# A gated cross-attention and mixture-of-experts block on one core: another order of the turns, and the last group's one-hot rows made on ScalarE

## The chip, the core and the metric

The kernel runs on one NeuronCore of a Trainium2 chip. The core has TensorE (PE in the profile), VectorE (DVE), ScalarE (ACT), GpSimd (POOL) and SyncE (SP), each with an instruction stream of its own; they meet through semaphores only. The metric is device time in microseconds (us) of one launch; lower is better.

## The reference

`x` is 4 batches of 1024 rows of 256 numbers. Two residual steps follow each other:

```
x = x + tanh(g_xattn) * cross_attention(layernorm(x), ctx)      # 77 keys per batch, W and b behind it
x = x + tanh(g_ffn)   * moe(layernorm(x))
# cross_attention: softmax(q k^T / 16), masked by position, times ctx, then @ W.T + b
# moe: logits = x @ router_w.T; the best 2 of 8 experts, weights renormalised
#      g, u = x @ w_gate[e].T, x @ w_up[e].T;  y = (silu(g) * u) @ w_down[e].T
```

The kernel computes each expert only for the rows that chose it, so it needs a list of rows per expert before the second step can begin.

## The kernel before

**Stage 1, attention and routing.** The 4096 rows are cut into 8 groups of 512 rows (4 tiles of 128), two groups to a batch. The groups go through a software pipeline written out by hand, in turns that are numbered k = 0 to 7. In turn k, DVE adds the attention result of group k to its rows (`add_rows`, L893), takes the first choices of the router (`lg`, `m8`, `mi`, `oh`), and prepares the softmax of group n = k + 2 (`maxima`, `refine`, `negated_maxima`). ACT sums squares for the two layer norms (`sum_squares`, `sum_squares2`), computes the inverse square root (`inverse_sqrt`) and the exponentials of group n (`exponentials`, L607). PE does in turn k: `attention(k+1)`, the value product of a later batch (`values`, L1154), products that nothing reads (`keep_busy`, L1096, one is a 128x512 product of ones), `transpose_exp(k+2)` (L1160), `scores(k+4)` (L1118 and L1121) and `ranks(k)` (L1177 to L1181), which counts how many earlier rows chose the same expert. In turn k, POOL adds the two choices (`picks`), which `ranks` waits for, and writes the normalised rows. SP loads `x` and `xT` of later groups, and stores rows.

**The list.** For each of 64 units (32 tiles, two choices) DVE makes a one-hot matrix of the low 7 bits of the rank, times a code of the row: `at_lows` (L842) compares, `coded` (L852) multiplies. After the last turn the expert's start is added and `at_tile` (L1008) is made, a one-hot matrix over 78 list columns. PE multiplies the two (L1227) and so adds up the list, in 64 products of 78 columns. A row of the first half has a positive code and one of the second half a negative code; DVE turns the sum into a row number (`sign`, `size`, `shift`, `idx`, L1014 to L1022). POOL then gathers rows by indirect DMA (L504).

**Stage 2, the experts.** Pairs of tiles, 34 of them in this input, go through the gate, up and down products, each split in three parts of float32 precision, and are added to the output by indirect DMA (L516). This stage isn't touched by the change.

The order is fixed by the order of the code on each engine, and each engine takes its instructions strictly in turn. A DVE instruction that needs the result of an earlier one waits for it by `after(...)`. In the order of before, the last group's tail on DVE is:

```
at_lows(last_group - 1, 0, 4); share(last_group); wait counts and ranks
nti; at_lows(6, 4, 6); nts; at_lows(6, 6, 8); ntf; cum; coded(6); start; own_ranks(7); starts; ...
at_tile x3; at_lows(7, 0, 8); coded(7); at_tile
```

Of the kernel before, what the change touches and what calls it, by code (L numbers as in the profile page):

```python
# [55 lines left out]
def moe_flamingo(nc, x, xT, ctx_rows, ctxT, lens, g_x, g_f, w_rows, wT, b_row, b_col, router, weights, out):  # L56
# [3 lines left out]
    with es:  # L60
# [51 lines left out]
        code = sb("code", [P, GROUPS, TOPK, G], F16, a)  # L112
        pad_row = sb("pad_row", [P, 1], F32, a)
# [42 lines left out]
        sign = sb("sign", [P, TILES], F32, a)  # L156
        size = sb("size", [P, TILES], F32, a)
        none = sb("none", [P, TILES], F32, a)
        shift = sb("shift", [P, TILES], F32, a)
# [87 lines left out]
        low_ready = sem("low_ready")  # L247
        counts_ready = sem("counts_ready")
# [167 lines left out]
        def _(pool):  # L416
# [25 lines left out]
            gp.iota(code[:, 0:GROUPS // 2], [[G * P, GROUPS // 2], [0, TOPK], [P, G]], base=1, channel_multiplier=1, **exact)  # L442
            gp.iota(code[:, GROUPS // 2:], [[-G * P, GROUPS // 2], [0, TOPK], [-P, G]], base=-1, channel_multiplier=-1, **exact)
            gp.iota(pad_row[:], [[1, 1]], base=N + 1, channel_multiplier=1, **exact)
# [112 lines left out]
        def _(act):  # L557
# [121 lines left out]

            nc.scalar.preload_act_table_set("silu_and_others")  # L680
# [37 lines left out]
        def _(dve):  # L718
# [167 lines left out]
            for k in range(GROUPS):  # L886
# [13 lines left out]
                summed = mark(tt(out=lg1[:], in0=lg0[:], in1=sr[:, q], op=ALU.add))  # L900
                add_rows(1).then_inc(rows_added, 1)
                after(summed)
                ts(negmean2[:, q], lg1[:, :, NE], -1.0 / D, None, ALU.mult).then_inc(negmean2_ready, 1)
# [4 lines left out]
                if k == 0:  # L908
# [11 lines left out]
                    values(1)  # L920
                    after(squared)
                else:
                    share(k - 1)
                if n + 1 < GROUPS:
                    negated_means(n + 1)
# [3 lines left out]
                if k > 0:  # L929
                    own = own_ranks(k - 1)  # L930
                    at_lows(behind, 2, 4)
                    ranked = unit_ranks(k - 1, own)
                    at_lows(behind, 4, 6)
                    masked = low_bits(k - 1, ranked)
                    at_lows(behind, 6, 8)
                    low_places(k - 1, masked)
                dve.wait_ge(ssq2_ready, k + 1)
                if more:
                    dve.wait_ge(ssq_ready, n)
# [26 lines left out]
                if k < 2:  # L966
                    values(k + 2)
# [3 lines left out]
            at_lows(last_group - 1, 0, 4)  # L971
            share(last_group)
            dve.wait_ge(counts_ready, 1)

            dve.wait_ge(ranks_ready, GROUPS)
            counted = mark(ts(nti[:], L[:, COUNTS:COUNTS + NE], float(PT - 1), None, ALU.add))
            at_lows(last_group - 1, 4, 6)
# [3 lines left out]
            at_lows(last_group - 1, 6, 8)  # L981
            after(counted)
            counted = mark(v.tensor_copy(ntf[:], nts[:]))
            after(counted)
            counted = mark(v.tensor_tensor_scan(cum[:], one8[:], ntf[:], 0.0, ALU.mult, ALU.add))
            coded(last_group - 1)
            after(counted)
            begun = mark(tt(out=start[:], in0=cum[:], in1=ntf[:], op=ALU.subtract))
            dve.wait_ge(chosen, GROUPS)
            own = own_ranks(last_group)  # L990
# [3 lines left out]
            ranked = unit_ranks(last_group, own)  # L994
            after(begun)
            begun = mark(v.tensor_reduce(first[:], starts[:], axis=AX.X, op=ALU.add))
            masked = low_bits(last_group, ranked)
            high_bits = mark(v.tensor_single_scalar(high[:], rank[:], P.bit_length() - 1, ALU.logical_shift_right))
            low_places(last_group, masked)
            after(begun)  # L1000
            after(high_bits)
            after(mark(tt(out=col[:], in0=first[:], in1=high[:], op=ALU.add)))
            side = [P, CHUNK // 2, TILES, 2]
            for c in range(UNITS // CHUNK):
                if c == UNITS // CHUNK - 1:
                    at_lows(last_group, 0, CU)
# [339 lines left out]
```

## Time and profile before

| what | value |
|---|---|
| median of 3 runs | 424.16 us (423.8 to 424.55) |
| profiled execution | 426.31 us, with a span of 424.6 us |
| mean granted TensorE clock | 0.991 |
| busy shares of the span | PE 97%, DVE 74%, ACT 66%, POOL 66% |
| stage 1, to the last store of `at_tile` | 0 to 97.4 us |
| list to the first transposed tile | 97.4 to 104 us |
| stage 2 | 104 us to the end |

PE's busy time holds 152 products that nothing reads (`W<-ones`, 36.5 us), beside those written to `ET`, so its share doesn't tell what bounds stage 1. In that stage the order of the waits does. The columns of a timeline row are: start, duration, engine, line, operation, tensors, shape, count, and in brackets how long the engine sat idle before it and who released it.

### The profile page before, as it was taken

How to read it: one execution, taken by the hardware profiler on the slowest of the kernel's cores; microseconds unless marked ns; L12 is line 12 of the kernel's file. 1: busy time of each engine (PE TensorE's matmuls, PEld its weight loads, DVE VectorE, ACT ScalarE, POOL GpSimd, SP SyncE). 2: the span in 40 equal slices, each digit the busy share in tenths (PEclk: the TensorE clock that was granted, in tenths of full speed). 3: DMA queues.
4: the chain of work that ended last, by engine and by line, in shares of the span. 5: the costliest groups of instructions: out<-in, count | busy, mean ns of one | idle time of the engine just before them, and what ended most of it. 6: DMA issues, size and time to landing. Idle time of an engine off the chain costs nothing.

```text
span 424.6 us, 9945 instructions
## 1 busy us (share of the span) xinstructions
PE 410.6 (97%) x3249; PEld 378.0 (89%) x3249; DVE 314.2 (74%) x694; ACT 281.7 (66%) x569; POOL 278.8 (66%) x269
## 2 busy tenths in 40 slices
PE   7999899998999999999999999999999999999993
PEld 2887775544999999999999999999999999999993
DVE  6557999986687777677777777777777776777772
ACT  2468877513576767777767766777767677767673
POOL 7004754754367677777777776677777777677775
PEclk9899999999999999999999999999999999999998
DMA  6846967751786777733334333434333434333433
GB/s 185 298 154 203 298 204 245 260 197 48 244 215 146 167 170 170 177 64 50 59 54 62 64 62 50 61 52 63 69 57 50 63 51 66 68 53 50 63 55 64
DMA packets 34624, 50.25 MB, mean 118 GB/s; under 512 B 3846, under 2 KB 26023, under 8 KB 34599
## 3 DMA queue, kind: packets, MB, share of 16 engines
q0 software_dynamic: 13440, 19.19, 27.1%
q1 hardware_dynamic: 19815, 29.84, 22.2%
q10 hardware_dynamic: 1344, 0.92, 0.7%
q8 instruction: 11, 0.18, 0.2%
q14 instruction: 14, 0.11, 0.1%
HBM read 32.24 MB, written 17.70 MB: 118 GB/s over the span
## 4 chain that ended last, share of the span: by engine, by line
PE 47%; POOL 23%; issue 15%; DVE 7%; ACT 3%; POOLq 2%; DMA 2%; ACTq 0%; DVEq 0%
POOL out_rows L516 15%; PE GT L1247 11%; PE UP L1247 11%; PE Y L1275 10%; POOL xt L504 7%; PE S L1121 4%; PE W L1096 3%; PE O L1170 2%; PE XT L1237 2%; ACT ex L607 2%; DMA out_rows<-y,idx 1%; PE ET L1096 1%; DVE at_low L842 1%; POOLq L533 1%; POOLq L60 1%
## 5 line engine op out<-in xcount | busy, mean ns | idle before, releaser
L516 POOL DMA_INDIRECT out_rows<-y,idx x68 | 159.6, 2347 | 65.6 <-ACT y L678 52.1
L1039 DVE TENSOR_TENSOR gu<-raw,gu 128x1024 fp32r<-128x1024 f32 x70 | 85.8, 1226 | 62.3 <-ACT gu L654 58.9
L1247 PE MATMUL GT<-xtT,gu 128*128 128x256 f32 x828 | 113.6, 286 | 0.4 <-DVE gu L1039 0.4
L1247 PE MATMUL UP<-xtT,gu 128*128 128x256 f32 x828 | 110.6, 283 | 0.0
L1247 PEld LDWEIGHTS GT<-xtT,gu 128*128 128x128 f32 x828 | 103.8, 191 | 0.8 <-DVE gu L1039 0.7
L1247 PEld LDWEIGHTS UP<-xtT,gu 128*128 128x128 f32 x828 | 104.3, 192 | 0.0
L1275 PE MATMUL Y<-dn,hT 128*128 128x256 f32 x816 | 103.6, 283 | 0.0
L1275 PEld LDWEIGHTS Y<-dn,hT 128*128 128x128 f32 x816 | 100.4, 192 | 0.1
L504 POOL DMA_INDIRECT xt<-xn_rows,idx x74 | 74.3, 1004 | 29.3 <-issue 22.2
L654 ACT CAST gu<-raw 128x1024 fp32r x68 | 70.9, 1042 | 30.7 <-PE UP L1247 28.5
L1060 DVE TENSOR_TENSOR hid<-hid,UP 128x512 f32<-128x512 f32 x68 | 46.5, 684 | 9.7 <-PE UP L1247 9.7
L667 ACT ACTIVATE hid<-GT 128x512 f32<-128x512 f32 x69 | 40.9, 593 | 11.3 <-PE GT L1247 10.0
L662 ACT CAST xtT<-XT 128x512 fp32r<-128x512 f32 x36 | 21.1, 587 | 40.4 <-issue 33.6
L1039 DVE TENSOR_TENSOR hT<-hid,hT 128x512 fp32r<-128x512 f32 x68 | 46.5, 684 | 0.2
L671 ACT CAST hT<-hid 128x512 fp32r<-128x512 f32 x68 | 42.0, 618 | 1.5 <-DVE hid L1060 1.5
L1039 DVE TENSOR_TENSOR dn<-raw,dn 128x1024 fp32r<-128x1024 f32 x35 | 42.7, 1219 | 0.0
L1096 PE MATMUL W<-ones 128*128 128x512 bf16 x152 | 36.5, 390 | 1.3 <-POOL ones L419 1.1
L678 ACT ACTIVATE y<-Y,xt 128x256 f32<-128x256 f32 x68 | 32.2, 475 | 5.9 <-PE Y L1275 5.2
L658 ACT CAST dn<-raw 128x1024 fp32r x34 | 35.6, 1048 | 0.0
L1039 DVE TENSOR_TENSOR xtT<-XT,xtT 128x512 fp32r<-128x512 f32 x36 | 24.9, 691 | 10.1 <-ACT xtT L662 7.0
L473 POOL TENSOR_TENSOR picks<-oh 128x32 bf16<-128x32 bf16 x8 | 2.1, 258 | 43.0 <-DVE oh L961 43.0
L1096 PEld LDWEIGHTS W<-ones 128*128 128x128 bf16 x152 | 14.5, 100 | 17.3 <-issue 1.9
(168 smaller groups left out, 395.7 us busy)
## 6 DMA issues: line engine op xcount, KB each, us to landing
raw<-in_weights SPq DMA_DIRECT2D x32, 384.0 KB
xn_rows<-pay SPq DMA_DIRECT2D x8, 528.0 KB, 3.3
xTg<-in_xT SPq DMA_DIRECT2D x8, 512.0 KB, 3.9
xg<-in_x SPq DMA_DIRECT2D x8, 512.0 KB, 5.9
out_rows<-xg SPq DMA_DIRECT2D x8, 512.0 KB, 4.0
xt<-xn_rows,idx POOLq DMA_INDIRECT x74
out_rows<-y,idx POOLq DMA_INDIRECT x68
kr<-in_ctx_rows SPq DMA_DIRECT2D x1, 308.0 KB
```

What stands on the lines that cost most here:

```text
L504: gp.indirect_dma_start(out=xt[:, 2 * s + t, :], out_offset=None, in_=xn_rows, in_offset=bass.IndirectOffsetOnAxis(ap=idx[:, 2 * j + t:2 * ...
L516: gp.indirect_dma_start(out=out, out_offset=bass.IndirectOffsetOnAxis(ap=idx[:, 2 * j + t:2 * j + t + 1], axis=0), in_=y[:, j % 2, t, :], ...
L654: nc.scalar.copy(gu[:, 0, q], gate_up_of(e, q)).then_inc(gu_high[q], 1)
L658: nc.scalar.copy(dn[:, 0, b], down_of(e)).then_inc(dn_high, 1)
L667: nc.scalar.activation(hid[:, q].rearrange("p h t -> p (h t)"), GT[:, q], ACT.Silu).then_inc(silu_ready, 1)
L671: nc.scalar.copy(hT[:, 0, 2 * q:2 * q + 2], hid[:, q]).then_inc(hid_high, 1)
L678: nc.scalar.mul(y[:, s % 2, t], Y[:, t, 0:D], xt[:, 2 * s + t, bass.ds(e + CW, 1)]).then_inc(y_ready, 1)
L1039: return tt(out=out, in0=whole, in1=high.bitcast(F32), op=ALU.subtract)
L1060: tt(out=wide, in0=wide, in1=UP[:, q], op=ALU.mult).then_inc(hid_ready, 1)
L1096: mm(bank[:], ones[:], ones[:].unsqueeze(1).to_broadcast([P, G, P]), start=True, stop=True)
L1247: last = mm(bank[:, h * PT:(h + 1) * PT], gu[:, pw, q, c, w, h * P:(h + 1) * P], xtT[:, b, px, c], start=(h == 0 and c == 0 and n == 0), s ...
L1275: last = mm(Y[:, t, 0:D], hT[:, px, 2 * q + c, t * P:(t + 1) * P], dn[:, pw, b, q, c * D:(c + 1) * D], start=(q == 0 and c == 0 and px == ...
```

## The change

- `values` of batches 2 and 3 goes, on PE, from behind `attention` to behind `scores`; on DVE the copy of batch k + 1 goes behind `negated_maxima` of turn k (k = 0, 1, 2).
- `ranks(k)` goes from behind `scores(k+4)` to right behind `transpose_exp(k+2)`.
- The products that nothing reads: 7 and 1 in place of 4 and 3 around the first transposes; behind `attention`, none at k = 0 and 3 at k > 0 in place of 10 and 5; at the end of a turn 2 from k = 3 on, in place of 4 from k = 2 on; 13 in place of 18 behind the last `ranks`.
- On DVE `share(k-1)` goes between `lg1` and `negmean2`, and `negmean2` ahead of `add_rows(1)`; `negated_means(n+1)` and `low_places` go behind `ve`.
- In the tail, `at_lows` and `coded` of group 6 go ahead of the wait for the counts, and the chain of group 7's ranks goes first. The one-hot rows of group 7 leave DVE: ACT makes them by 8 `Square` and 8 `Relu` instructions on 128x128 elements.
- The codes are changed so that group 7 has a positive one, and the row number takes 4 DVE instructions in place of 5. Two small `iota` instructions more on POOL.

The core of the diff:

```diff
@@ ScalarE, behind the last turn
+            act.wait_ge(places_ready, GROUPS)
+            act.wait_ge(pool_consts, 4)
+            for u in range(CU):
+                nc.scalar.activation(apart[:, u], iota_p[:, :, 0], ACT.Square, bias=low_last[:, u:u + 1], scale=-1.0
+                                     ).then_inc(apart_ready, 1)
+            for u in range(CU):
+                act.wait_ge(apart_ready, u + 1)
+                last = nc.scalar.activation(at_low[:, (UNITS - CU + u) // 2, :, u % 2], apart[:, u], ACT.Relu,
+                                            bias=code_last[:, 0, u % G:u % G + 1], scale=code_last[:, 1, u % G:u % G + 1])
+            last.then_inc(last_low_ready, 1)
             nc.scalar.preload_act_table_set("silu_and_others")
@@ VectorE, turn k
                 summed = mark(tt(out=lg1[:], in0=lg0[:], in1=sr[:, q], op=ALU.add))
+                if k > 0:
+                    share(k - 1)
+                after(summed)
+                ts(negmean2[:, q], lg1[:, :, NE], -1.0 / D, None, ALU.mult).then_inc(negmean2_ready, 1)
                 add_rows(1).then_inc(rows_added, 1)
...
+                if n + 1 < GROUPS:
+                    negated_means(n + 1)
+                if k > 0:
+                    low_places(k - 1, masked)
                 coded(behind)
                 refine(n)
                 if more:
                     after(reduced)
                     negated_maxima(n)
+                if k + 1 < BATCH:
+                    values(k + 1)
@@ TensorE
-            keep_busy(4, W)
+            keep_busy(7, W)
             transpose_keys(0, M)
-            keep_busy(3, W)
+            keep_busy(1, W)
...
                 attention(k + 1)
-                if k < 2:
-                    values(k + 2)
-                keep_busy(10 if k == 0 else 5, ET)
+                if k > 0:
+                    keep_busy(3, ET)
                 if k + 2 < GROUPS:
                     transpose_exp(k + 2)
+                ranks(k)
                 if k + 4 < GROUPS:
                     scores(k + 4)
                 else:
                     keep_busy(9, W)
-                ranks(k)
-                if k >= 2:
-                    keep_busy(4, W)
+                if k + 2 < BATCH:
+                    values(k + 2)
+                if k >= BATCH - 1:
+                    keep_busy(2, W)
...
-            keep_busy(18, W)
+            keep_busy(13, W)
...
+                    if u == UNITS - CU:
+                        pe.wait_ge(last_low_ready, 1)
+                    else:
+                        pe.wait_ge(low_ready, u // CU + 1)
```

TensorE in turn 0, from behind the value product of `attention(1)` on. Before, the value product of batch 2 and ten products that nothing reads stand ahead of the transposes of `ex` (to `ET`):

```order
L1170 MATMUL O<-vw,eT 128x256
L1154 MATMUL W<-wT_sb,ctxT_sb 77x265 x2
L1096 MATMUL ET<-ones 128x512 x10
L1160 MATMUL ET<-ident,ex 77x128 x4
L1118 MATMUL S<-krow,qrow 128x384
L1121 MATMUL S<-krT,xTg 128x96 x8
L1177 MATMUL L<-carry,ones 128x32
```

The same stretch of the changed kernel:

```order
L1188 MATMUL O<-vw,eT 128x256
L1178 MATMUL ET<-ident,ex 77x128 x4
L1195 MATMUL L<-carry,ones 128x32
L1197 MATMUL L<-picks,ones 128x24
L1197 MATMUL L<-picks,ones 128x16
L1197 MATMUL L<-picks,ones 128x8
L1199 MATMUL L<-picks,tri 128x32
L1136 MATMUL S<-krow,qrow 128x384
L1139 MATMUL S<-krT,xTg 128x96 x8
L1172 MATMUL W<-wT_sb,ctxT_sb 77x265 x2
```

The transposes now stand right behind the attention, then the ranks (to `L`), the scores (to `S`) and the value product.

VectorE in the middle of turn 3 (one at a later turn reads the same up to turn 5), before; `ve` is what ACT's inverse square root waits for:

```order
L807 RECIPROCAL rw<-ed 128x4
L775 TENSOR_SCALAR negmean<-S 128x4
L778 TENSOR_REDUCE mx<-S 128x4
L782 COPY sr<-S 128x36
L813 TENSOR_TENSOR po<-oh,L 128x64
L842 TENSOR_TENSOR at_low<-iota_p,low 128x256
L818 TENSOR_REDUCE rank<-po 128x8
L842 TENSOR_TENSOR at_low<-iota_p,low 128x256
L823 TENSOR_SCALAR low_i<-rank 128x8
L842 TENSOR_TENSOR at_low<-iota_p,low 128x256
L827 CAST low<-low_i 128x8
L940 TENSOR_SCALAR ve<-ssq 128x8
```

And in the changed kernel, from `mx` on:

```order
L796 TENSOR_REDUCE mx<-S 128x4
L800 COPY sr<-S 128x36
L831 TENSOR_TENSOR po<-oh,L 128x64
L860 TENSOR_TENSOR at_low<-iota_p,low 128x256
L836 TENSOR_REDUCE rank<-po 128x8
L860 TENSOR_TENSOR at_low<-iota_p,low 128x256
L841 TENSOR_SCALAR low_i<-rank 128x8
L860 TENSOR_TENSOR at_low<-iota_p,low 128x256
L956 TENSOR_SCALAR ve<-ssq 128x8
L793 TENSOR_SCALAR negmean<-S 128x4
L845 CAST low<-low_i 128x8
L870 TENSOR_TENSOR at_low<-at_low,code 128x1024
```

Three small instructions (`rw`, `negmean`, `low`) left the stretch ahead of `ve`; two of them now stand right behind it.

VectorE in the tail of the changed kernel, from the last turn's end to the list:

```order
L860 TENSOR_TENSOR at_low<-iota_p,low 128x512 x2
L870 TENSOR_TENSOR at_low<-at_low,code 128x1024
L825 RECIPROCAL rw<-ed 128x4
L831 TENSOR_TENSOR po<-oh,L 128x64
L1001 TENSOR_SCALAR nti<-L 128x8
L836 TENSOR_REDUCE rank<-po 128x8
L1005 TENSOR_SCALAR nts<-nti 128x8
L841 TENSOR_SCALAR low_i<-rank 128x8
L1008 CAST ntf<-nts 128x8
L1011 CAST low_last<-low_i 128x8
```

`low_last`, which ACT's 16 new instructions wait for, is the sixth small instruction behind the wait for the counts, and no one-hot work of group 6 or 7 stands between that wait and `at_tile` any more.

## Rows read from the trace of the kernel before

**Rows 1.** Timeline of PE, start to the second scores:
```profile
1.06 6.74 PE L1096 MATMUL W<-ones 128*128 128x512 bf16 x24 [1.06 <-POOL ones L419]
...
9.32 0.36 PE L1105 MATMUL M<-ident,kr 85*128 85x85 f32 x2 [1.52 <-DVE kr L752]
...
10.53 3.58 PE L1121 MATMUL S<-krT,xTg 128*128 128x96 f32 x16
...
16.53 2.02 PE L1121 MATMUL S<-krT,xTg 128*128 128x96 f32 x16
```

**Rows 2.** Windows: stretch, its length, busy by engine, PEclk, DMA share, GB/s
```profile
13.00:14.00 1.00, 1.00 (x7) 1.00 (x7) 0.73 (x6) 0.16 (x1) 0.00 (x0) 0.50 1.03 373
...
96.00:98.00 2.00, 0.72 (x20) 0.59 (x17) 1.41 (x2) 0.00 (x0) 0.00 (x0) 1.00 0.03 8
```

**Rows 3.** Timeline of PE in turn 0:
```profile
29.45 0.28 PE L1169 MATMUL M<-vw,eT 77*128 77x9 f32 x2
...
32.07 1.06 PE L1154 MATMUL W<-wT_sb,ctxT_sb 128*77 128x265 f32 x4
32.96 2.32 PE L1096 MATMUL ET<-ones 128*128 128x512 bf16 x10
35.12 0.60 PE L1160 MATMUL ET<-ident,ex 128*77 128x128 f32 x4
```

**Rows 4.** Timeline of DVE, turns 0 to 4, value copy and turn starts:
```profile
29.65 0.49 DVE L858 SCALAR_TENSOR_TENSOR vw<-W,gates,bias 77x265 f32<-77x265 f32 x1 [2.68 <-PE W L1154]
...
30.61 0.16 DVE L940 TENSOR_SCALAR ve<-ssq 128x8 f32<-128x8 f32 x1
...
34.33 0.18 DVE L896 TENSOR_TENSOR lg<-M,rg 128x36 f32<-128x36 f32 x1
...
43.06 0.18 DVE L896 TENSOR_TENSOR lg<-M,rg 128x36 f32<-128x36 f32 x1
...
58.65 0.20 DVE L896 TENSOR_TENSOR lg<-M,rg 128x36 f32<-128x36 f32 x1
```

**Rows 5.** Timeline of ACT in turn 0, end of the squares of group 2:
```profile
28.42 0.19 ACT L584 ACTIVATION_READ_ACCUMULATOR squares<-xg,negmean 128x1 f32 x1
```

**Rows 6.** SP's issue of x for group 4, and x's landing time:
```profile
29.67 0.51 SPq L323 DMA_DIRECT2D xg<-in_x  x1
```
```profile
xg<-in_x SPq DMA_DIRECT2D x8, 512.0 KB, 5.9
```

**Rows 7.** Timeline of DVE in turn 4:
```profile
63.04 0.16 DVE L940 TENSOR_SCALAR ve<-ssq 128x8 f32<-128x8 f32 x1
...
64.31 0.16 DVE L798 SCALAR_TENSOR_TENSOR nb<-mx,rt 128x4 f32<-128x4 f32 x1
...
66.27 0.18 DVE L803 RECIPROCAL rg<-rs 128x4 f32<-128x4 f32 x1 [0.28 <-ACT ex L607]
```

**Rows 8.** Timeline of ACT in turn 4:
```profile
64.56 0.40 ACT L607 ACTIVATE ex<-S,nb,rt 128x77 f32<-128x77 f32 x1
```

**Rows 9.** Timeline of DVE, the tail:
```profile
89.35 0.17 DVE L976 TENSOR_SCALAR nti<-L 128x8 int32<-128x8 f32 x1 [0.73 <-PE L L1181]
...
93.13 2.24 DVE L1008 TENSOR_TENSOR at_tile<-iota_t,col 128x1248 f16<-128x1248 f16 x3
95.29 0.69 DVE L842 TENSOR_TENSOR at_low<-iota_p,low 128x1024 f16<-128x1024 f16 x1
96.01 0.69 DVE L852 TENSOR_TENSOR at_low<-at_low,code 128x1024 f16<-128x1024 f16 x1
96.62 0.80 DVE L1008 TENSOR_TENSOR at_tile<-iota_t,col 128x1248 f16<-128x1248 f16 x1
```

**Rows 10.** Timeline of PE, the list and the first tile:
```profile
97.48 0.79 PE L1227 MATMUL L<-at_tile,at_low 128*128 128x78 f16 x16 [1.28 <-DVE at_tile L1008]
...
103.93 0.66 PE L1285 MATMUL XT<-ident,xt 128*128 128x128 f32 x4
```

**Rows 11.** Groups by line and shape, ACT:
```profile
L593 ACT ACTIVATE squares<-xg,negmean 128x256 f32<-128x256 f32 x32 | 15.9, 497 | 2.9 <-DVE negmean L903 2.8
```

More of the change, by code:

```diff
@@ L112, in moe_flamingo @@
         code = sb("code", [P, GROUPS, TOPK, G], F16, a)
+        code_last = sb("code_last", [P, 2, G], F32, a)
+        low_last = sb("low_last", [P, CU], F32, a)
+        apart = sb("apart", [P, CU, P], F32, a)
         pad_row = sb("pad_row", [P, 1], F32, a)
@@ L247, in moe_flamingo @@
         low_ready = sem("low_ready")
+        apart_ready = sem("apart_ready")
+        last_low_ready = sem("last_low_ready")
         counts_ready = sem("counts_ready")
@@ L900, in _ @@
                 summed = mark(tt(out=lg1[:], in0=lg0[:], in1=sr[:, q], op=ALU.add))
-                add_rows(1).then_inc(rows_added, 1)
+                if k > 0:
+                    share(k - 1)
                 after(summed)
                 ts(negmean2[:, q], lg1[:, :, NE], -1.0 / D, None, ALU.mult).then_inc(negmean2_ready, 1)
+                add_rows(1).then_inc(rows_added, 1)
                 add_rows(2).then_inc(rows_added, 1)
@@ L919, in _ @@
                     squared = mark(ts(ssq[:, 0, G // 2:G], xmv[:, G // 2:G, 1], float(D), None, ALU.mult))
[L920 to L925, printed above, removed]
                 if more:
@@ L975, in _ @@
             dve.wait_ge(ranks_ready, GROUPS)
+            dve.wait_ge(chosen, GROUPS)
+            own = own_ranks(last_group)
             counted = mark(ts(nti[:], L[:, COUNTS:COUNTS + NE], float(PT - 1), None, ALU.add))
-            at_lows(last_group - 1, 4, 6)
+            ranked = unit_ranks(last_group, own)
             after(counted)
             counted = mark(ts(nts[:], nti[:], PT.bit_length() - 1, 1, ALU.logical_shift_right, ALU.logical_shift_left))
-            at_lows(last_group - 1, 6, 8)
+            masked = low_bits(last_group, ranked)
             after(counted)
             counted = mark(v.tensor_copy(ntf[:], nts[:]))
+            after(masked)
+            v.tensor_copy(low_last[:], low_i[:]).then_inc(places_ready, 1)
             after(counted)
             counted = mark(v.tensor_tensor_scan(cum[:], one8[:], ntf[:], 0.0, ALU.mult, ALU.add))
-            coded(last_group - 1)
+            high_bits = mark(v.tensor_single_scalar(high[:], rank[:], P.bit_length() - 1, ALU.logical_shift_right))
             after(counted)
             begun = mark(tt(out=start[:], in0=cum[:], in1=ntf[:], op=ALU.subtract))
-            dve.wait_ge(chosen, GROUPS)
-            own = own_ranks(last_group)
             after(begun)
@@ L1013, in _ @@
             listed = L[:, LIST:LIST + TILES]
[L1014 removed]
+            lower = mark(ts(lift[:], listed, 0.0, float(N // 2 - 1), ALU.is_lt, ALU.add))
             empty = mark(ts(none[:], listed, 0.0, pad_row[:], ALU.is_equal, ALU.mult))
[L1016 to L1017 removed]
+            after(lower)
+            lifted = mark(stt(out=size[:], in0=listed, scalar=1.0, in1=lift[:], op0=ALU.mult, op1=ALU.add))
             after(empty)
[L1019 to L1022 removed]
+            after(lifted)
+            tt(out=idx[:], in0=size[:], in1=none[:], op=ALU.add).then_inc(idx_ready, 1)
             empty = mark(ts(second_empty[:], L[0:1, LIST:LIST + TILES].rearrange("p (j t) -> p j t", t=2)[:, :, 1], 0.0, 16.0,
```

35 lines of the change are left out of this document (11 added, 24 removed).

## The prediction

> **What bounds the kernel now.** I read the chain of waits first. It shows stage 2 as one unbroken chain of 34 pairs, and stage 1 as a mixture of engines, so whatever ends stage 1 earlier ends the kernel earlier, as long as nothing in stage 2 hangs on a load of stage 1. The weight loads of later experts are issued once the first tiles have landed, so they move along. I then read each engine's timeline from 0 to 112 us. Three places matter.
>
> *The start.* PE runs 24 unread products to 7.8 us, sits idle for 1.52 us until the centred keys come, and then needs 3.58 us for the first scores; the second scores, the same 16 products, take 2.02 us [rows 1]. The windows say why: the granted clock is 0.50 (1.2 GHz) there [rows 2], and it is 1.00 nearly everywhere else.
>
> *Turns 0 to 2.* PE is the late engine. In turn 0 the value product of batch 2 and ten unread products lie between the attention, which ends at 32.07, and the transposes at 35.12 [rows 3]. And DVE holds back everything behind the copy of batch 1's values, for which it waits 2.68 us; `ve` comes only at 30.61 [rows 4], while the squares that it needs end at 28.61 [rows 5].
>
> *Turns 3 on.* The ring is DVE and ACT: `lg` 58.65, `ve` 63.04, `nb` 64.31, `ex` from 64.56, `rg` 66.27, and `lg` 0.29 later: 7.91 us a turn [rows 4, 7, 8]. DVE itself idles 0.28 in it, so it can't shrink much. *The tail* is a DVE chain: `nti` 89.35, `at_tile` from 93.13, then 1.33 us of one-hot rows between the third and the fourth `at_tile`, for which PE waits 1.28 [rows 9, 10].
>
> **The change part by part.**
>
> *Start.* Seven products instead of four push the end of the unread work from 7.8 to about 8.45 and cut the idle time to about 0.9; of three products behind the transposes two go. If the clock stays at 1.00, the first scores take about 2.0 in place of 3.58: 1.56 gained. Two products fewer at 0.216 each (ten take 2.16 from 32.96 to 35.12 [rows 3]), partly replaced by the wait for ACT's copy of the keys, give another 0.3. Everything behind is PE work in one row up to the attention of group 0, so both reach turn 0: 1.9. If the clock still falls, 0.35 is left. The trace bounds it from both sides: 1.52 idle, followed by the fall; 1.28 idle ahead of the last list products with the clock at 1.00 throughout [rows 2, 10]. 0.9 is on the safe side of the second, so I take 1.9 and keep 0.35 as the low end.
>
> *Turn 0.* `ve` no longer waits for the value copy: 28.7 in place of 30.6. Then, with the gaps of [rows 7, 8], `nb` at about 30.0 and `ex` of group 2 from about 30.3 to 32.0 (1.7 for four). The attention of group 1 ends at 32.07, the transposes follow at once, not at 35.12. Turn 1 starts on DVE when `oh` is written (`nb` + 1.5, and 0.4 for the moved value copy) and the attention is done: about 32.3 for 34.33, 2.0 gained.
>
> *Turn 1.* PE does transposes (0.6), ranks (0.2), scores (2.3), value product (0.9), so that attention of group 2 starts at 36.0. ACT has the squares of turn 1 done at 35.8, hence `ve` at 35.85 (four squares and a copy of `eT` behind 33.1), `nb` 37.2, `ex` to 39.1, turn 2 at 39.4 for 43.06: 3.65. *Turn 2* carries a value copy too (0.4, of which about 0.15 shows, since DVE idles only 0.28), turn 3 starts at about 47.4, and turn 4 at 55.3 for 58.65 [rows 4]: 3.4.
>
> *Turns 3 to 7.* `rw`, `negmean` and `low` leave the stretch ahead of `ve`: 0.14 + 0.15 + 0.13, less a stall of about 0.2 where `negmean2` now has only one small instruction between it and its input. So `ve` is 0.2 earlier; but `negmean` and `low` now lie ahead of `refine`, and `nb` moves back by the same 0.2. `ex` follows `nb` by 0.04 at best, where it now follows by 0.09 [rows 7, 8]. Between 0 and 0.06 a turn: I take 0.05 for 4 turns, 0.2 in all. Below nothing: if POOL, which works beside DVE, stretches them, 0.1 a turn is lost. The unread products that go here shorten PE where it waits anyhow, for `ex` and for `rows_added`; the scores come well ahead of `negmean` now. Both ends: 3.1 to 3.8 for all the turns; I take 3.5 with the last term.
>
> *Tail.* Ahead of the counts DVE now does all of group 6's one-hot rows: 0.34 + 0.34 + 0.6 from about 87.7, so that it is ready at 89.15, about when PE's ranks arrive (89.1): the first wait is covered by work that was needed anyway. `nti` to `at_tile` was 3.78 [rows 9]; group 6's one-hot rows, 0.2 + 0.49 + 0.59 on the same timeline, leave it, and about 0.2 of waiting that they covered comes back. So `at_tile` starts about 2.75 behind `po`, at 92.0 in place of 93.13. Four of them in a row at 0.72 end at 94.95; before, 97.42 [rows 9]. That is 2.47. ACT gets `low_last` at about 90.2. A `Square` has half the columns of [rows 11] (497 ns for 256); 0.83 ns a column off gives 0.39, and less 0.09 of overlap 0.3 each. A `Relu` has two pointer operands as `ex` has, 0.40 for 77 columns [rows 8], so 0.35 to 0.39 each. 8 x 0.3 + 8 x 0.37 = 5.4, so ACT ends at 95.6. PE needs it for its last 8 products only, which would start at 95.4. It costs 0.2 (0 to 0.5), so the tail gives 2.25, between 1.9 and 2.5. Were each ACT instruction as long as the 0.497 of the wide one, ACT would end at 98.1, and the tail would give nothing; that is the far end.
>
> The Trainium skill, "ScalarE: Activation LUTs", under "What ACT_TABLE_LOAD costs", gives 280 ns + 0.833 ns a column with one pointer operand, 93 ns for another and 93 ns of overlap. The trace agrees (493 ns for 256 columns by that rule; 497 in the row). By it the 16 come to 5.45 us, the same sum. Its "Rules for kernel authors" say to use VectorE for `relu` and not ScalarE, which speaks against this edit: DVE does the same rows in 1.33 us of trace time. By that rule alone the tail would get worse; the row says that ACT stands idle there, so I follow the row.
>
> *The row number.* One dependent instruction fewer on DVE, 0.2. PE goes on at 103.93 without idle time of its own behind its unread products [rows 10], so what the gather gains is hidden: 0. The gather also waits for the last store of normalised rows, which moves by the turns' gain, not by the tail's; the DMA engines were nearly idle from 96.0 on [rows 2], so it has landed in time by about 1 us.
>
> **Sum.** 1.9 + 3.5 + 2.25 = 7.65. The profiled execution would go from 426.31 to 418.7; the median lies 2.15 under the profiled time, so 416.5; I say 416.7, since the ring is full and small stalls add.
>
> **Rivals.**
>
> *The clock still falls at the start.* For it: the seven products end 0.9 ahead of the keys, still a gap, and fewer products follow. Against it: the 1.28 gap without a fall. 6.1 gained, 418.1.
>
> *The turns give back part.* x of group 4 is issued at 29.67 and lands 5.9 later, 35.6 [rows 6]; in my schedule it is needed at 36.4, 0.8 later. Group 5's is as tight, as its issue hangs on the POOL store of group 0. If loads or DVE's full row take half of the turns' gain (1.8), and ACT's row the far part of its price (1.0), 419.4.
>
> *The clock falls in the turns.* This is the slower side. The unread products go from 9 to 5 a turn or to 3 (turns 1 and 2), and PE will sit 1.1 to 1.3 us ahead of the transposes. At 1.2 GHz PE's work of a turn, 5.9 us (transposes, ranks, scores, attention), stretches by 3.58/2.02 to 10.4 and becomes the bound: 2.5 us more a turn. It decides from three turns on; over six it is +15, less 6: 433. Against it: the 1.28 of idle time at the list went by at full clock [rows 2, 10], and what is left idle in a turn is no longer.
>
> **How the numbers follow.** The forecast (7.65, with its own range 415.6 to 417.6) has 0.52; the clock fall at the start 0.24; part given back 0.13; the clock in the turns 0.06; 0.05 is left for an unseen wait that leaves about no change. About 0.2% (0.85 us) is what a measurement of this kernel can tell from no change. The first three are all faster, so 0.91 with a part of the rest; 0.03 the same; 0.06 slower. The range 415.0 to 419.8 holds the first three cases nearly whole.
>
> **What would show it.** The first scores at about 2.0 us and PEclk 1.00 from 10 to 14; turn starts (`lg`) near 30.4, 37.5, 53.4 (my 32.3, 39.4, 55.3 less 1.9); the first `at_tile` 2.75 behind `po`, four without a gap; ACT's 16 instructions in 5.4 us with no table load among them; the last list products released by ACT, not by DVE. It is wrong if PEclk shows 0.5 between 10 and 80 us, if a turn from the third on takes over 8.0 us, or if `squares` waits for a load of x.

## Result and the profile after

| | before | changed kernel |
|---|---|---|
| median of 6 runs each | 424.26 us (423.79 to 424.55) | 422.35 us (420.82 to 423.1) |
| ratio | | 0.9948, 95% interval 0.9934 to 0.9962 |
| profiled execution, its span | 426.31, 424.6 us | 420.82, 419.1 us |
| mean granted TensorE clock | 0.991 (profiled) | 0.985 (profiled), 0.980 to 0.982 in the other five |

The change gains 1.9 us, where 7.6 were forecast; 422.35 us is above the forecast's 415.0 to 419.8. All of the granted clocks are lower than before. Single executions of the kernel before have such a clock too (3 of the 64 that ran beside the experiments, 0.981 or 0.982, at 430.8 to 431.6 us); the ratios leave out executions over 1.5% above a kernel's fastest.

Timeline of PE in the changed kernel, columns as in [rows 1]:

```profile
10.70 2.03 PE L1139 MATMUL S<-krT,xTg 128*128 128x96 f32 x16
...
52.73 0.66 PE L1178 MATMUL ET<-ident,ex 128*77 128x128 f32 x4 [1.22 <-ACT ex L614]
...
53.71 2.98 PE L1139 MATMUL S<-krT,xTg 128*128 128x96 f32 x16
...
57.62 1.20 PE L1188 MATMUL O<-vw,eT 77*128 77x256 f32 x2
...
63.74 1.06 PE L1178 MATMUL ET<-ident,ex 128*77 128x128 f32 x4
...
89.88 3.08 PE L1249 MATMUL L<-at_tile,at_low 128*128 128x78 f16 x64 [1.48 <-DVE at_tile L1027]
...
98.93 0.33 PE L1307 MATMUL XT<-ident,xt 128*128 128x128 f32 x1 [0.36 <-DMA xt<-xn_rows,idx]
```

The first scores take 2.03 us, as forecast for them (3.58 in [rows 1]). But from the scores of turn 3 to the transposes of turn 4 everything on PE is long: the scores 2.98, the pair of products to `O` 1.20 where the pair before it has 0.68, the transposes 1.06 for 0.66. Ahead of that PE sat idle for 1.22 us, waiting for `ex`. The windows of the same kernel (columns as in [rows 2]) say what it is:

```profile
13.00:14.00 1.00, 1.00 (x12) 0.95 (x11) 0.93 (x8) 0.28 (x2) 0.00 (x0) 1.00 1.06 386
52.00:54.00 2.00, 1.26 (x12) 1.05 (x13) 1.62 (x11) 2.00 (x10) 1.22 (x6) 1.00 0.93 267
54.00:55.00 1.00, 1.00 (x10) 1.00 (x9) 1.00 (x4) 1.00 (x4) 1.00 (x3) 0.78 0.77 272
55.00:64.00 9.00, 9.00 (x31) 7.00 (x31) 6.33 (x42) 5.37 (x25) 6.08 (x16) 0.50 0.64 208
64.00:65.00 1.00, 1.00 (x11) 0.82 (x10) 1.00 (x4) 0.17 (x1) 0.76 (x4) 0.60 0.00 0
```

The granted clock is 0.50 (1.2 GHz) from some 54.5 to 64.8 us, and 1.00 around it. PE is busy for the whole of it, while DVE falls to 6.33 of 9 us. It begins some 1.8 us after the idle 1.22 has ended (at 52.73).

DVE in the changed kernel, turn starts (against [rows 4]) and the tail (against [rows 9]):

```profile
27.10 0.17 DVE L956 TENSOR_SCALAR ve<-ssq 128x8 f32<-128x8 f32 x1 [0.97 <-ACT squares L591]
...
30.83 0.20 DVE L914 TENSOR_TENSOR lg<-M,rg 128x36 f32<-128x36 f32 x1 [0.26 <-PE O L1188]
...
37.50 0.20 DVE L914 TENSOR_TENSOR lg<-M,rg 128x36 f32<-128x36 f32 x1
...
53.00 0.20 DVE L914 TENSOR_TENSOR lg<-M,rg 128x36 f32<-128x36 f32 x1
...
62.70 0.20 DVE L914 TENSOR_TENSOR lg<-M,rg 128x36 f32<-128x36 f32 x1 [2.29 <-PE O L1188]
...
70.98 0.20 DVE L914 TENSOR_TENSOR lg<-M,rg 128x36 f32<-128x36 f32 x1
...
85.72 0.22 DVE L831 TENSOR_TENSOR po<-oh,L 128x64 f32<-128x64 bf16 x1
...
89.01 2.96 DVE L1027 TENSOR_TENSOR at_tile<-iota_t,col 128x1248 f16<-128x1248 f16 x4
92.99 0.24 DVE L1034 TENSOR_SCALAR lift<-L 128x78 f32<-128x78 f32 x1 [1.01 <-PE L L1249]
```

The turns start at 30.83, 37.50 and 53.00, where 30.4, 37.5 and 53.4 were forecast. Then turn 4 takes 9.70 us, with DVE waiting 2.29 for PE, and turn 5 takes 8.28. `ve` of turn 0 (27.10) no longer waits for a value copy, only for the squares. In the tail the four `at_tile` stand in a row, but the first comes 3.29 behind `po`, not 2.75.

ACT in the tail of the changed kernel:

```profile
86.84 2.44 ACT L691 ACTIVATE apart<-iota_p,low_last 128x128 f32<-128x128 f16 x8 [3.27 <-DVE low_last L1011]
89.19 3.23 ACT L695 ACTIVATE at_low<-apart,code_last 128x128 f16<-128x128 f32 x8
92.43 1.28 ACT L698 ACT_TABLE_LOAD   x1
```

The 16 instructions take 5.58 us, and the table load follows them.

### The profile page after: what moved, and what is told of

Its sections match the earlier page's. It is cut to its first block, busy times and chain, and to the rows that moved or that the text cites. A ratio compares the mean times of both kernels' runs of the same rounds, so it can differ in the third digit from the quotient of the medians.

```text
span 419.1 us, 9883 instructions
## 1 busy us (share of the span) xinstructions
PE 406.4 (97%) x3211; PEld 377.1 (90%) x3211; DVE 311.4 (74%) x690; ACT 287.4 (69%) x585; POOL 280.6 (67%) x271
## 4 chain that ended last, share of the span: by engine, by line
PE 45%; POOL 24%; issue 16%; DVE 6%; DMA 3%; ACT 2%; POOLq 2%; SPq 0%; ACTq 0%; DVEq 0%
POOL out_rows L523 15%; PE GT L1269 11%; PE UP L1269 11%; PE Y L1297 10%; POOL xt L511 8%; PE W L1114 3%; PE S L1139 3%; PE O L1188 2%; PE XT L1259 2%; DMA xg<-in_x 2%; DVE xg L911 1%; DMA out_rows<-y,idx 1%; POOLq L60 1%; POOLq L540 1%; ACT ex L614 1%
## 5 line engine op out<-in xcount | busy, mean ns | idle before, releaser
L511 POOL DMA_INDIRECT xt<-xn_rows,idx x74 | 75.2, 1017 | 27.4 <-issue 22.2
L1114 PE MATMUL W<-ones 128*128 128x512 bf16 x136 | 34.4, 407 | 1.3 <-POOL ones L424 1.1
L1114 PEld LDWEIGHTS W<-ones 128*128 128x128 bf16 x136 | 13.6, 104 | 17.3 <-issue 3.7
```

Of the source, the lines that this page charges most:

```text
L511: gp.indirect_dma_start(out=xt[:, 2 * s + t, :], out_offset=None, in_=xn_rows, in_offset=bass.IndirectOffsetOnAxis(ap=idx[:, 2 * j + t:2 * ...
L1114: mm(bank[:], ones[:], ones[:].unsqueeze(1).to_broadcast([P, G, P]), start=True, stop=True)
```

## The experiments

Ratios are to the kernel before, run beside each experiment on the same chip. Undisturbed means a mean granted clock of 0.994 or more over the whole execution. The first four ran together, the next four on another chip, then two and then one on a third; across these groups the ratios are to be compared, not the times.

**The kernel before, unchanged.**

> The kernel of before, word for word, for the granted clock and the span of each run. Theory A (the profiled execution of before, 426.31, was one with the clock fall at the start, and most executions don't have it): the six runs spread by about 2 us in two groups, those at 424 with a higher mean clock than the profiled one's 0.991, and a profile of a run at 424 shows the first scores at about 2.0 us. Rival B (the start is the same each time and the profiler or the chip adds 2): every run's clock is 0.991 and the first scores take 3.6 us at 424 too.

424.88 us (424.56 to 426.3, 11 runs), ratio 0.9997 (0.9985 to 1.0009), clocks 0.996 to 0.999. The fall at the start that [rows 1, 2] show isn't there. But neither theory is right as it was put: the longer executions, 425.8 and 426.3, have a clock of 0.998 too, so something other than this fall lengthens them. PE in the profiled execution, which is the one at 426.3 (span 424.6):

```profile
4.45 4.61 PE L1096 MATMUL W<-ones 128*128 128x512 bf16 x16
9.37 0.37 PE L1105 MATMUL M<-ident,kr 85*128 85x85 f32 x2 [0.31 <-DVE kr L752]
...
10.58 2.02 PE L1121 MATMUL S<-krT,xTg 128*128 128x96 f32 x16
...
102.34 0.66 PE L1285 MATMUL XT<-ident,xt 128*128 128x128 f32 x4
```

The 24 unread products last until 9.06, not 7.80, so the gap ahead of the keys is 0.31 and not 1.52. The other four profiled executions with the old start (in four of the kernels below) have gaps from none to 1.14 there, and all have first scores of 2.02. All of stage 1 is 1.6 us earlier than in [rows 4, 10] (first transposed tile 102.34 for 103.93). Yet the span is the same 424.6. From the first down product (`Y`) to the end of the span every profiled execution of this study takes 310.0 to 310.7 us, so the 1.6 us went between the two, in what I call the opening of stage 2: first transposed tile to first `Y`. It is 10.3 us in the profiled execution of before and 12.0 here.

**Only the start's products.**

```diff
-            keep_busy(4, W)
+            keep_busy(7, W)
             transpose_keys(0, M)
-            keep_busy(3, W)
+            keep_busy(1, W)
```

> Before, with 7 and 1 unread products around the first transposes in place of 4 and 3, nothing else. If the start's term was right as a mean: 1.5 to 1.9 faster, 422.4. Theory A: only executions that would have fallen gain, so 0.2 to 0.8 faster on the median, about 423.7, with the first scores at 2.0 us and clock 0.995.

425.49 us (423.73 to 427.32, 11 runs), ratio 1.0015 (0.9998 to 1.0032). Both sizes expected, 1.5 to 1.9 and 0.2 to 0.8 us faster, are missed, and the start's term is nothing: the turns begin 0.07 to 0.14 us earlier than in the unchanged kernel's trace (turn 0 at 22.22 for 22.29, turn 4 at 56.97 for 57.08), and the time doesn't follow.

**The change with the old number of unread products in the turns and behind the last ranks.**

```diff
@@ against the changed kernel
-                    keep_busy(3, ET)
+                    keep_busy(5, ET)
...
-                    keep_busy(2, W)
+                    keep_busy(4, W)
...
-            keep_busy(13, W)
+            keep_busy(18, W)
```

> The changed kernel with the unread products of the turns as before: 5 behind attention in place of 3 (k > 0), 4 at a turn's end from k = 3 on in place of 2, 18 in place of 13 behind the last ranks. Theory A (the turns' gain is eaten by a clock fall in the turns that the thinner PE row lets in): clock 1.00 in all turns, mean clock of 0.99 or more, no turn over 8.0 us, and 418 to 419.5. Rival (the fall doesn't hang on the unread products but on the order, which bunches PE's work): the clock falls as before this edit, 421.5 to 423.

419.32 us (418.65 to 420.08, 4 runs), ratio 0.9869 (0.9855 to 0.9884), clocks 0.995 to 0.997. With this row nothing falls, and the change gains 5.5 us.

**The kernel before with fewer unread products in the turns, nothing else.**

```diff
@@ against the kernel before
-                keep_busy(10 if k == 0 else 5, ET)
+                keep_busy(10 if k == 0 else 3, ET)
...
-                if k >= 2:
-                    keep_busy(4, W)
+                if k >= 3:
+                    keep_busy(2, W)
```

> Before, with fewer unread products in the turns (3 in place of 5 from k = 1 on; none at the end of turn 2 and 2 from turn 3 on in place of 4), the order as it was. Theory A (fewer products alone let the clock fall): a stretch at 0.50 in the turns, mean clock about 0.98, 425 to 428. Rival (it takes the new order too): clock as before and 424.2 within 0.5.

429.24 us as the median of 11 runs, but from 424.13 to 436.9, with clocks from 0.999 down to 0.960; ratio 1.0063 (1.0032 to 1.0095) with the five longest left out. Nine of the eleven have a clock of 0.983 or less, at 428.8 us and above; the other two are at 424.13 and 425.17. The last wait ahead of the fall in its profiled execution (433.55 us), and the windows:

```profile
49.18 0.66 PE L1160 MATMUL ET<-ident,ex 128*77 128x128 f32 x4 [1.50 <-ACT ex L607]
```

```profile
50.00:60.00 10.00, 10.00 (x41) 8.50 (x41) 7.09 (x46) 6.77 (x30) 4.78 (x16) 0.51 0.69 222
60.00:70.00 10.00, 10.00 (x43) 8.28 (x41) 5.96 (x39) 5.34 (x22) 2.92 (x8) 0.50 0.56 186
70.00:80.00 10.00, 9.66 (x47) 6.18 (x45) 7.01 (x42) 5.78 (x26) 4.25 (x13) 0.80 0.51 164
```

No step of the change is in it but the thin row of unread products. In the old order that alone costs 4 us in four of its executions and 7 to 12 in five. The wait for `ex` is 1.50 us, where the unchanged kernel has 1.09 at this place and stays at full clock. So the thin row is enough for a fall; the next four runs were for the sizes.

**The changed kernel, unchanged.**

> The changed kernel word for word, beside the run with the old unread products (419.3) and on the same chip as this call's others. Theory A (all of what is missing is the clock in the turns): every run has a mean clock of 0.980 to 0.985, the median is 421.5 to 423, and the profile shows 8 to 14 us at 0.50 between 45 and 75 us. Rival (the first six runs were odd): clock 0.995 and 419.5.

421.72 us (8 runs), ratio 0.9923 (0.9888 to 0.9959). The runs are of two kinds: 417.85, 418.1 and 418.81 at clocks of 0.994 to 0.998, and five from 421.43 to 422.86 at 0.980 or 0.981. With the six runs of the result, 11 of 14 executions fall, by their mean clocks; that every one would, as expected, isn't so. The profiled one is undisturbed (span 417.1). PE and the windows in it:

```profile
53.03 0.66 PE L1178 MATMUL ET<-ident,ex 128*77 128x128 f32 x4 [1.21 <-ACT ex L614]
```

```profile
54.00:64.00 10.00, 9.18 (x62) 6.87 (x61) 9.52 (x53) 9.09 (x38) 7.30 (x19) 1.00 0.71 234
```

The same place, the same idle time of 1.21 us, and the clock stays at 1.00. So the gap of this length doesn't decide the fall by itself.

**Only the new order of the turns**, on PE and DVE, with the old 5 and 4 unread products, the old start and the old tail.

```diff
@@ against the kernel before, TensorE (VectorE as in the change)
-                if k < 2:
-                    values(k + 2)
-                keep_busy(10 if k == 0 else 5, ET)
+                if k > 0:
+                    keep_busy(5, ET)
...
+                ranks(k)
...
-                ranks(k)
-                if k >= 2:
+                if k + 2 < BATCH:
+                    values(k + 2)
+                if k >= BATCH - 1:
                     keep_busy(4, W)
```

> Before, with the new order of the turns on PE and DVE, the unread products of the turns at the old numbers (5, 9, 4; none in turn 0), the old start and the old tail. The forecast's term: 3.5 faster, 421.2 where before is 424.7. If stage 2's opening (gathers and weight loads side by side) takes part of what comes earlier, 2.5 or less.

419.27 us (419.02 to 419.66, 5 runs), ratio 0.9881 (0.9867 to 0.9895): 5.0 us. DVE in turn 4 of this kernel:

```profile
52.93 0.20 DVE L896 TENSOR_TENSOR lg<-M,rg 128x36 f32<-128x36 f32 x1
...
53.66 0.17 DVE L905 TENSOR_SCALAR negmean<-lg 128x4 f32<-128x4 f32 x1
...
56.75 0.16 DVE L938 TENSOR_SCALAR ve<-ssq 128x8 f32<-128x8 f32 x1
...
58.25 0.16 DVE L798 SCALAR_TENSOR_TENSOR nb<-mx,rt 128x4 f32<-128x4 f32 x1
...
60.18 0.18 DVE L803 RECIPROCAL rg<-rs 128x4 f32<-128x4 f32 x1 [0.24 <-ACT ex L607]
60.46 0.20 DVE L896 TENSOR_TENSOR lg<-M,rg 128x36 f32<-128x36 f32 x1
```

And three lines of the unchanged kernel: the same instruction in turns 3 and 4, and the wait for the scores in turn 3.

```profile
50.17 0.16 DVE L903 TENSOR_SCALAR negmean<-lg 128x4 f32<-128x4 f32 x1
...
51.82 0.16 DVE L775 TENSOR_SCALAR negmean<-S 128x4 f32<-128x4 f32 x1 [0.37 <-PE S L1121]
...
58.08 0.41 DVE L903 TENSOR_SCALAR negmean<-lg 128x4 f32<-128x4 f32 x1
```

A turn is 7.53 us, not 7.91. From `lg` to `ve` it is 3.82 for 4.39 [rows 4, 7], from `ve` to `nb` 1.50 for 1.27, and the rest is as it was. I had forecast 0.2 less and 0.2 more for the first two. I had charged a stall of 0.2 for `negmean2` with only one small instruction ahead of it; the trace has no such stall, and the instruction itself takes 0.17 where it took 0.41. It isn't the place alone that made it long: in the old order it takes 0.35 to 0.42 in five turns and 0.16 in three, in the new one 0.15 to 0.17 in all eight. In turn 3, where the old order has 0.16, DVE waits 0.37 for the scores instead, and that wait is gone too.

**Only the new tail**, with 18 unread products behind the last ranks (the edit is the tail's part of the change: VectorE, ScalarE, the codes and the wait of the last eight list products).

```diff
@@ against the kernel before
+            for u in range(CU):
+                nc.scalar.activation(apart[:, u], iota_p[:, :, 0], ACT.Square, bias=low_last[:, u:u + 1], scale=-1.0
...
+            for u in range(CU):
+                act.wait_ge(apart_ready, u + 1)
```

> Before, with the new codes and the new tail (one-hot rows of group 7 on ACT, group 6's ahead of the counts, four instructions to the row number), 18 unread products behind the last ranks, the old turns and the old start. The forecast's term: 2.25 faster, 422.5. Rival of the forecast (ACT is the late engine of the tail): 1.0 faster. If the list's last products are released by DVE at four at_tile of 0.74, ACT costs nothing.

422.25 us (421.97 to 422.96, 6 runs), ratio 0.9954 (0.9941 to 0.9967): 2.0 us. DVE and PE there:

```profile
87.89 0.22 DVE L831 TENSOR_TENSOR po<-oh,L 128x64 f32<-128x64 bf16 x1
...
91.15 2.97 DVE L1025 TENSOR_TENSOR at_tile<-iota_t,col 128x1248 f16<-128x1248 f16 x4
```

```profile
92.02 2.63 PE L1246 MATMUL L<-at_tile,at_low 128*128 128x78 f16 x56 [0.36 <-DVE at_tile L1025]
94.91 0.49 PE L1246 MATMUL L<-at_tile,at_low 128*128 128x78 f16 x8 [0.26 <-ACT at_low L695]
```

The last eight products are released by ACT and wait 0.26 for it, near the 0.2 of the forecast. This run moves the one-hot rows and reorders DVE's tail at once; no run separates the two. The first `at_tile` comes 3.26 behind `po`, and 0.42 us earlier than in the unchanged kernel (91.57). The list ends at 95.40 for 96.71, with the turns 0.06 later: 1.4 in the profiled executions, 2.0 in the medians. Where the other 0.6 lies wasn't traced.

**The change with PE's gaps filled.**

```diff
@@ against the changed kernel
-                    keep_busy(3, ET)
+                    keep_busy(3 if k == 1 else 6 if k == 2 else 8, ET)
...
-            keep_busy(13, W)
+            keep_busy(18, W)
```

> The changed kernel with 3, 6 and from turn 3 on 8 unread products behind attention, which the waits for ex (0.5 to 2.0 us) have room for, 2 at a turn's end as it is, and 18 behind the last ranks. Theory A: clock at 1.00 as with the old numbers, and 419.3 or 0.2 to 0.5 less, since PE's attention starts up to 0.4 earlier. Rival (the two at the turn's end matter, not those behind attention): the clock falls, 421 to 423.

418.79 us (417.28 to 420.61, 6 runs), ratio 0.9875 (0.9851 to 0.9898), clocks 0.995 to 0.998. PE has no idle time left over 0.2 us from 35 to 70. The turns are shorter than anywhere (last `lg` 73.74, for 74.82 in the undisturbed changed kernel), and the first transposed tile comes at 95.64. But the kernel isn't faster than that one's 417.85 to 418.81: the opening of stage 2 takes 10.8 us here and 10.2 there. The first tile is 0.64 earlier than there, but the third tile's transposes start at 104.54 in both, as its gather is waited for:

```profile
95.64 0.66 PE L1307 MATMUL XT<-ident,xt 128*128 128x128 f32 x4 [0.39 <-DMA xt<-xn_rows,idx]
...
104.54 0.65 PE L1259 MATMUL XT<-ident,xt 128*128 128x128 f32 x4 [0.99 <-DMA xt<-xn_rows,idx]
```

**The same, with the weight loads of experts 2 and 3 behind the third tile.**

```diff
@@ SyncE, against the filled kernel
-            load_weights(2, range(PARTS))
-            load_weights(3, range(PARTS))
             for s in range(2, AHEAD):
                 sp.wait_ge(tile_loaded[s], 32)
+            load_weights(2, range(PARTS))
+            load_weights(3, range(PARTS))
```

> The changed kernel with TensorE's gaps filled (3, 6 and 8 unread products behind the attention, 18 behind the last ranks, which gave 418.8 us), and SP issues the weight loads of experts 2 and 3 once the third tile of gathered rows has landed, where it issued them once the first two had. Theory A: the opening of stage 2 (first transposed tile to first down product, 10.8 us there, 9.8 in the changed kernel) is long because the later tiles' gathers share the DMA engines with the weight loads. Then it falls to about 9.8 and the kernel to 417.3 to 418.0. Theory B: the opening is set by TensorE and by the copies on DVE and ACT; then nothing changes (within 0.4 us of 418.8). Theory C: the weights of expert 2 now come too late and stage 2 waits for them: slower than 418.8.

418.17 us (417.27 to 419.26, 5 runs), ratio 0.9844 (0.9821 to 0.9866): the lowest ratio of the study. The wait for the third tile is gone (its transposes start at 103.40), the opening takes 10.2 us, and the span is 416.4 for 416.8. Theory A has the direction right in the traces; by times alone the difference from the filled kernel is within the spread of both (their intervals overlap, and they ran on different chips).

**Five more unread products at one place.**

```diff
@@ against the changed kernel
-                    keep_busy(3, ET)
+                    keep_busy(8 if k == 3 else 3, ET)
```

> The changed kernel with five more unread products in one place only, behind the attention of turn 3, where TensorE waited 1.22 us for ex and the granted clock fell about 1 us later. Theory A: that one gap lets the clock fall. Then no execution falls (granted clock of 0.994 and more in all) and the time is that of the undisturbed executions of the changed kernel, 417.9 to 418.8 us. Theory B: it is the thinned row as a whole. Then the clock still falls in part of the executions, at another turn, and their times stay near 421 to 423.

419.08 us (418.58 to 419.85, 4 runs), ratio 0.9866 (0.9843 to 0.989), clocks 0.994 to 0.997. The place and a later wait in its profiled execution, and a window:

```profile
52.85 0.66 PE L1178 MATMUL ET<-ident,ex 128*77 128x128 f32 x4
...
67.91 0.66 PE L1178 MATMUL ET<-ident,ex 128*77 128x128 f32 x4 [1.09 <-ACT ex L614]
```

```profile
54.00:64.00 10.00, 9.18 (x61) 6.87 (x62) 9.51 (x54) 8.94 (x37) 7.30 (x18) 1.00 0.70 229
```

None of four executions falls, where 11 of 14 did without the edit. Were the edit without effect, and 11 of the 18 fell all the same, four drawn at random would all be undisturbed about once in 90 times; that is strong but not certain, and the 14 ran in other groups than the four, eight of them on another chip. The kernels with the old fill or the filled gaps, which thicken this place too, have 15 more executions without a fall. So Theory A holds as far as shown: filling the place ahead of turn 3's transposes is enough. Other waits for `ex` stay in this kernel, up to 1.09 us, at full clock.

**The kernel before with the late weight loads alone** (the same edit of SyncE).

> The kernel before with one edit: SP issues the weight loads of experts 2 and 3 once the third tile of gathered rows has landed, where it issued them once the first two had. In the kernel before, unchanged, the opening of stage 2 takes 12.0 us in a usual execution: ScalarE copies the second transposed tile 2.4 us after TensorE has made it (idle 3.68 us, released by remote), and VectorE and TensorE wait behind it. Theory A: this idle time is an effect of the weight loads that start at 105.5 us, just as ScalarE gets there. Then it goes, the opening falls to 10.0 to 10.6 and the kernel gains about 1.5 us (423.1 to 423.5). Theory B: it has to do with ScalarE's own stream and not with the DMA traffic. Then ScalarE's copy stays at about 109.8 and the time within 0.5 us of the kernel before.

424.23 us (423.84 to 431.47, 11 runs), ratio 0.9988 (0.9978 to 0.9998): 0.5 us, less than the 1.5 of theory A. Two of the eleven have a clock of 0.982 and 431.4 us, as one of 14 of the unchanged kernel beside them. Its profiled execution looks as theory A has it. ScalarE's copy of the second transposed tile, which TensorE has ready at 107.38, and the stretch around it, in the unchanged kernel:

```profile
109.82 0.59 ACT L662 CAST xtT<-XT 128x512 fp32r<-128x512 f32 x1 [3.68 <-remote]
```

```profile
108.00:112.00 4.00, 2.90 (x23) 2.46 (x21) 1.29 (x2) 1.76 (x3) 0.79 (x1) 1.00 1.02 401
```

With the late loads:

```profile
107.45 0.59 ACT L662 CAST xtT<-XT 128x512 fp32r<-128x512 f32 x1 [1.47 <-PE XT L1237]
```

```profile
108.00:112.00 4.00, 4.00 (x35) 3.88 (x34) 3.64 (x6) 2.69 (x5) 0.64 (x1) 1.00 0.81 227
```

The copy comes 0.2 us after the tile is there, the opening takes 9.8 us in place of 12.0, and the DMA engines move 227 GB/s and not 401 in the stretch. What ScalarE waited for in the unchanged kernel the trace calls remote. Two rows from the other traces keep this from being an answer. The first execution of the kernel before, with its early weight loads, has no such wait, and its opening takes 10.3 us (TensorE has this tile ready at 108.97):

```profile
109.72 0.58 ACT L662 CAST xtT<-XT 128x512 fp32r<-128x512 f32 x1 [1.99 <-PE XT L1237]
```

And in the changed kernel the DMA engines move 398 GB/s around the same copies, with ScalarE busy for 3.18 of 4 us and no remote wait:

```profile
104.00:108.00 4.00, 4.00 (x35) 3.86 (x35) 3.09 (x5) 3.18 (x5) 1.08 (x2) 1.00 1.00 398
```

The remote wait stands in three profiled executions, the unchanged kernel's and those of the runs with only the start's products and with fewer unread products, each with an opening of 12.0. That the late loads remove it isn't shown by one execution. Why the medians follow by only 0.5 us is open; the unchanged kernel's profiled execution was the longest of its eleven (426.3, median 424.88), so most executions probably have a shorter opening.

## Why the prediction was wrong, point by point

**The base and the start (1.9 forecast, 0 measured).** The step that failed first is the one that took the start's gain from the profiled execution and then set the median 2.15 under it. The fall at the start belonged to that execution: the 28 runs of the kernel before beside the first four experiments hold one with such a clock (0.991, at 426.26). In the other five profiled executions with the old start the gap is between none and 1.14 us with no fall, and the products alone give nothing. The fall cost that execution 1.6 us of stage 1, which the forecast took as a gain while it had set the base under it: counted twice. It isn't the only thing that lifts an execution to 426, though: the unchanged kernel's profiled execution got there without a fall, by an opening of 12.0 us. The sign that I asked for, first scores of 2.0 us, was seen and proves nothing, since the kernel before has it too.

**The turns (3.5 forecast, 5.0 measured).** The mechanism was right and the size too small. The starts of turns 1 and 2 came within 0.5 us of those forecast, and up to turn 3 the gain is 3.4 as forecast (45.54 for 49.17, less 0.27 from the start). What was mis-sized is the term for the turns from 3 on, 0.2 in all, where 1.35 came: from the start of turn 3 to that of turn 7 the new order takes 28.93 us (45.54 to 74.47) and the unchanged kernel 30.28 (49.17 to 79.45), 1.35 less, for the reasons under the turns' own run: a stall that I charged and that doesn't come, an instruction that takes 0.24 less in turns 4 to 6, and in turn 3 a wait of 0.37 for the scores that is gone. The possible wait for x, which I had as a rival, is nearly there: group 6's load lands at 49.87 in the changed kernel and its squares start at 49.89, with the inverse square root done at 49.9.

**The tail (2.25 forecast, 2.0 measured).** Near in the median, but partly by luck: the trace of the new tail alone gives 1.4, below the 1.9 that I had as the low end. The first `at_tile` was forecast 1.13 earlier and came 0.42 earlier. The row of DVE between `po` and `at_tile` is 3.3 us, not 2.75: I gave back 0.2 for waits that group 6's one-hot rows had covered, and the trace has about 0.6 (`nti` to `at_tile` 3.12, for 3.78 less 1.28 of those rows). ACT's 16 instructions take 5.58 us for 5.4. The Trainium skill, "ScalarE: Activation LUTs", under "What ACT_TABLE_LOAD costs", states figures from which I estimate 2.44 and 3.19 us for 8 in a row with one pointer operand and then 8 with two; the trace has 2.44 and 3.23, so it agrees. The Trainium skill's rule under "Rules for kernel authors" on the same page, to use VectorE for `relu`, spoke against an edit that gained 2.0 us together with DVE's new order. What the move to ACT gives by itself no run shows; ACT stood idle there, and PE waited 0.26 for it.

**The row number (0 forecast).** Hidden in the kernel before, but no longer: wherever turns and tail are both new, PE waits 0.2 to 0.4 us for the gather ahead of the first tile. Why the gather takes longer there (first `idx` to first tile 5.24 us in the changed kernel, 4.75 in the unchanged one) wasn't tried.

**The clock in the turns (chance 0.06 forecast, 11 of 14 executions).** This is the step that decides the miss: the overlap that I took for granted, that the unread products which go only shorten PE where it waits anyhow. I had the mechanism of what came: fewer unread products, PE idle 1.1 to 1.3 us ahead of the transposes (1.22 came), the scores and the attention long. I argued it away with 1.28 us of idle time at the list that went by at full clock [rows 10]. One place at which a gap went well says nothing of another: the same gap of 1.21 and 1.22 us in the same kernel is followed by a fall in one execution and by none in the next. The price a turn was about right, 2.2 us for turn 4 (7.52 to 9.70) where I had 2.5; the length was wrong, about 10 us in the profiled execution and not six turns. Turns 4 and 5 (8.28) lose 2.9 us in all. The medians of the two kinds of executions differ by 4.4 us (422.5 and 418.1). If the lower clocks of the other executions, 0.981 for 0.985, all come from the turns, they mean some 3 us more at half clock (an estimate, 0.004 x 420 / 0.5).

**The sum again.** On the chip where turns and tail were measured the unchanged kernel has 424.2; less 5.0 and 2.0 that is 417.3. The undisturbed executions of the changed kernel there stand at 417.85 to 418.81, 5.4 to 6.4 gained, and the fall brings most of them to 421.4 to 422.9. The repaired versions gain 5.5, 5.5 and 5.8 us, and 6.7 with the late weight loads. In the traces stage 1 does add up: the first transposed tile comes 4.8 us earlier by the turns and 1.4 by the tail, and 6.1 earlier in the undisturbed changed kernel, where the tail's and the turns' medians promise 7.0. So what doesn't add up seems to lie behind the first tile, in the opening of stage 2, where the gathered tiles, the weight loads and ScalarE's copies meet, and which took between 9.8 and 12.0 us over the profiled executions of this study. How much of that spread a kernel owns and how much is chance stays open.

## What to carry to other kernels

Before a gain is read from one profiled execution that lies above the runs, ask whether the thing to be gained is what sets it above them, and look at a second execution; if it is, the gain is counted from the median or from the profile, never from both. Unread products that only fill a wait can still be what keeps TensorE's clock up: when an edit shortens TensorE's row, put as many back as make up the gap ahead of the waits. Here that brought 422.4 us to 418.8, or 419.1 with one gap filled, within about 1 us of the executions without a fall, and it is tested in one run. And a gap that was harmless at one place bounds nothing at another.

## What the runs showed of the hardware

- The granted clock after the same idle time (1.21 and 1.22 us, the same instruction, the same kernel) fell in one profiled execution to 0.50 for some 10 us and stayed at 1.00 in another; by the mean clock (0.985 or less), 11 of 14 executions fell. With five products in that gap none of four did. Idle times of 1.48 and 1.51 us ahead of the list's products, in the undisturbed changed kernel and in the one with that gap filled, were followed by a clock of 1.00.
- The unread products of the first microseconds aren't of one length: 24 of them, from 1.06 on, lasted to 7.80 in one execution and to 9.06 in another (8 and 6 of them between 3 and 5 us), with a granted clock of 1.00 in the windows of both. The gap that follows is 1.52 or 0.31 us by that.
- The same small DVE instruction (128x4) took 0.35 to 0.42 us in five turns of the unchanged kernel and 0.16 in three, between two long instructions each time; behind a small one it took 0.15 to 0.17 in all eight. What makes the difference wasn't tested.
- A wait that the trace calls remote held ScalarE for 2.4 us after its input was there, in three profiled executions. With the weight loads issued later it didn't come, but neither did it in other executions with the early loads.
- Issuing the weight loads behind the third gathered tile took away a wait of 0.99 us for that tile in the one pair of traces that shows it.
